# A decoder of four layers: softmax sums by part, gates in bfloat16 parts, and one named activation table set

## The reference, cut to what matters

```python
a_comp = _masked_softmax(q . compressed keys * SCALE, comp_mask)   # 32 blocks of 16 keys
a_sel  = _masked_softmax(q . keys of the top 2 blocks, causal_sel) # 16 keys
a_win  = _masked_softmax(q . keys, last 32 keys only)              # window
# _masked_softmax: e = exp(s - max), zeros where all is masked; e / sum(e)
g = softmax(x @ Wg + bg)
out = (g[0] * a_comp@cv + g[1] * a_sel@vs + g[2] * a_win@v) @ Wo + bo
```

```python
gates = zeros(T, 8); gates[rows, top2] = softmax(top2 logits)
h = relu(xf @ Wd[e] + bd[e]);  y = 0.5 * (h @ Wu[e] + bu[e])
out = einsum('te,ted->td', gates, y)
```

## Time and profile before

| | us |
|---|---|
| runs | 2310.97 to 2317.59, median of three 2312.99 |
| profiled execution | 2319.51 |
| its span | 2317.3 |
| PE / DVE / ACT / POOL busy | 1874.7 (81%) / 1637.3 (71%) / 1048.1 (45%) / 620.0 (27%) |
| DVE's scans of l3_attn, L2505, 128 of them | 193.7 busy, 1.1 idle before |
| granted PE clock over the span | 0.855 of full |

### The profile page before, as it was taken

How to read it: one execution, slowest core, us unless ns; L and a number is a source line. 1 busy time by engine, 2 the same in 40 slices (tenths; PEclk the granted TensorE clock), 3 DMA queues, 4 the chain that set the end, 5 groups by cost and what they waited for, 6 DMA issues and landing times. The chain is left out here.

```text
span 2317.3 us, 31149 instructions
## 1 busy us (share of the span) xinstructions
PE 1874.7 (81%) x11250; PEld 1074.1 (46%) x11250; DVE 1637.3 (71%) x3694; ACT 1048.1 (45%) x1706; POOL 620.0 (27%) x532
## 2 busy tenths in 40 slices
PE   4788888879888989999997668678976676689974
PEld 2444554536363333577776646555532232243432
DVE  6666847666678878744537896984379979994656
ACT  1226656474743553743434434442264355426552
POOL 0002424242332010100003544620136635731000
PEclk8888998989897786999998888776687797889975
DMA  4001213040302000000000000000000000000000
GB/s 171 1 0 41 65 29 77 9 97 2 89 17 95 1 1 1 1 23 1 1 1 10 1 1 1 1 1 1 1 0 1 1 0 0 1 1 1 1 1 19
DMA packets 19223, 44.31 MB, mean 19 GB/s; under 512 B 5323, under 2 KB 7935, under 8 KB 18047
## 3 DMA queue, kind: packets, MB, share of 16 engines
q1 hardware_dynamic: 19071, 42.33, 6.5%
HBM read 17.15 MB, written 1.05 MB: 8 GB/s over the span
## 5 line engine op out<-in xcount | busy, mean ns | idle before, releaser
L2374 PE MATMUL lane_banks<-l_attn_lane_hc,base 128*128 128x512 f32 x256 | 161.2, 743 | 91.6 <-DVE l_attn_lane_hc L2514 91.2
L2456 POOL TENSOR_TENSOR l_attn_lane_u<-l_attn_lane_xp,l_attn_lane_bn 128x512 f32<-128x512 f32 x128 | 189.6, 1510 | 123.9 <-ACT l_attn_lane_bn L2427 107.2
L604 POOL TENSOR_SCALAR lane_next_rstd<-lane_next_mv 128x4 f32<-128x4 f32 x48 | 11.9, 248 | 699.7 <-DVE lane_next_mv L581 699.7
L2505 DVE TENSOR_TENSOR_SCAN l_attn_lane_h<-l_attn_lane_da,l_attn_lane_u 128x512 f32<-128x512 f32 x128 | 193.7, 1558 | 1.1 <-ACT l_attn_lane_da L2435 0.8
L1728 ACT ACTIVATE l_ffn_lane_hT<-lane_banks,weights 128x512 f32<-128x512 f32 x128 | 87.9, 687 | 145.1 <-PE lane_banks L1682 144.5
L1774 DVE SCALAR_TENSOR_TENSOR l_ffn_lane_eo<-lane_banks,l_ffn_lane_sel,l_ffn_lane_eo 128x128 f32<-128x128 f32 x224 | 63.0, 343 | 101.4 <-PE lane_banks L1704 100.9
L2374 PEld LDWEIGHTS lane_banks<-l_attn_lane_hc,base 128*128 128x128 f32 x256 | 56.8, 238 | 162.5 <-DVE l_attn_lane_hc L2514 127.5
L1526 ACT ACTIVATE l_attn_lane_ex<-lane_banks 128x512 f32<-128x512 f32 x160 | 84.1, 668 | 97.2 <-PE lane_banks L1440 96.5
L1704 PEld LDWEIGHTS lane_banks<-weights,l_ffn_lane_hT 128*128 128x128 f32 x1024 | 119.8, 192 | 15.9 <-issue 12.2
L1704 PE MATMUL lane_banks<-weights,l_ffn_lane_hT 128*128 128x128 f32 x1024 | 122.8, 276 | 0.9 <-DVE l_ffn_lane_eo L1774 0.9
L591 DVE TENSOR_SCALAR lane_rows<-x,lane_next_mv,lane_next_rstd 128x128 f32<-128x128 f32 x192 | 76.0, 465 | 38.8 <-POOL lane_next_rstd L605 38.6
(11 more groups left out here) (528 smaller groups left out, 4719.6 us busy)
## 6 DMA issues: line engine op xcount, KB each, us to landing
f_attn_lane_vb<-f_attn_lane_work SPq DMA_DIRECT2D x192, 64.0 KB, 2.0
weights<-packed SPq DMA_DIRECT2D x1, 4564.5 KB, 13.5
f_attn_lane_work<-f_attn_lane_work SPq DMA_DIRECT2D x64, 64.0 KB, 2.0
f_attn_lane_vb<-f_attn_lane_va SPq DMA_DIRECT2D x8, 512.0 KB, 4.6
f_attn_lane_vb<-f_attn_lane_va SPq DMA_DIRECT2D x8, 384.0 KB, 5.9
weights<-packed SPq DMA_DIRECT2D x1, 2320.0 KB, 9.7
weights<-packed SPq DMA_DIRECT2D x1, 2091.0 KB, 14.1
weights<-packed SPq DMA_DIRECT2D x1, 1263.0 KB, 5.4
```

Of the source, the lines that this page charges most:

```text
L2374: pe.matmul(ps(2 + c), w("ident"), hc[:, c, :], start=(n == 1), stop=(n == NS)).then_inc(*s.up("state_added"))
L2456: g.tensor_tensor(u[:, i % 3, :], dtx[:, c, :], bn[:, n % 2, :], ALU.mult).then_inc(*s.up("u_ready"))
L2505: v.tensor_tensor_scan(h[:, c, :], da[:, i % 3, :], u[:, i % 3, :], 0.0, ALU.mult, ALU.add).then_inc(*s.up("scanned"))
```

## The change

In `l2_attn`, maxima, sums, subtraction and POOL's multiplication each go straight over the three parts of `sc` (64, 32 and 16 keys) in three instructions; the intermediate tiles of seven places are gone. The guard against an empty part is one `max` with 0.5 in place of an `is_equal` and an addition. The gate multiplication writes the weights in one instruction. `shift` waits for the subtraction of the group before, `weigh` for its weights.

In `l2_ffn`, the gates are split into three bfloat16 parts whose sum is the float32 value, transposed and copied out as 24 rows, and spread by a bfloat16 matmul over these. `gateT` stays for L2252.

In `f0_attn` and `l3_attn`, a named table set, which holds Ln and Exp, is loaded once in each unit. The costs in `Meter` have no price for it.

```diff
-A2_PARTS = ((0, 4), (4, 6), (6, 7))
+A2_PARTS = ((0, 64, 2), (64, 96, 0), (96, 112, 1))
 # l2_attn
+    def part(g, i):
+        lo, hi, k = A2_PARTS[i]
+        return sc[:, g % 2, :, :, lo:hi].rearrange("p j g n -> p (j g) n"), hi - lo, k
 # POOL, weights(g)
-            g_.tensor_tensor(sevenths(g), sevenths(g), bci(wt7[...], 16), ALU.mult)
+            for i in range(3):
+                to, n, k = part(g, i)
+                last = g_.tensor_tensor(to, to, bci(wt[:, g % 2, :, k], n), ALU.mult)
 # DVE, shift(g)
-            st.link(v.tensor_reduce(mx7[...], sevenths(g), AX.X, ALU.max))
-            for i, (lo, hi) in enumerate(A2_PARTS):
-                st.step(v.tensor_reduce(mx[:, :, i], mx7[:, :, lo:hi], AX.X, ALU.max))
+            if g >= 1:
+                v.wait_ge(*s.at("shifted", g))
+            for i in range(3):
+                of, _, k = part(g, i)
+                st.step(v.tensor_reduce(mx[:, :, k], of, AX.X, ALU.max))
             st.wait()
-            for i, (lo, hi) in enumerate(A2_PARTS):
-                st.step(v.tensor_scalar(mx7[:, :, lo:hi], bci(mx[:, :, i], hi - lo), -1.0e20, None, ALU.max))
-            st.wait()
-            v.tensor_tensor(sevenths(g), sevenths(g), bci(mx7[...], 16), ALU.subtract)
+            st.link(v.tensor_scalar(mx[:, :, :], mx[:, :, :], -1.0e20, None, ALU.max))
+            for i in range(3):
+                to, n, k = part(g, i)
+                last = v.tensor_tensor(to, to, bci(mx[:, :, k], n), ALU.subtract)
 # DVE, weigh(g)
-            (reduce of sevenths, three reduces, is_equal, add, reciprocal, three gate products, three copies)
+            if g >= 1:
+                v.wait_ge(*s.at("weights_ready", g))
+            for i in range(3):
+                of, _, k = part(g, i)
+                st.step(v.tensor_reduce(sm[:, :, k], of, AX.X, ALU.add))
+            st.wait()
+            st.link(v.tensor_scalar(zero[:, :, :], sm[:, :, :], 0.5, None, ALU.max))
+            st.link(v.reciprocal(sm[:, :, :], zero[:, :, :]))
+            yield
+            if g >= 2:
+                v.wait_ge(*s.at("probs_ready", g - 1))
+            v.tensor_tensor(wt[...], sm[...], gl[...], ALU.mult)
 # l2_ffn, PE
+        pe.wait_ge(*s.at("parts_ready", 1))
+        for t in range(NT):
+            last = pe.transpose(ps(1).bitcast(BF16)[0:3 * E, tile(t)], gate16[:, t, :, :], net.w16("ident16"))
+        last.then_inc(*s.up("partsT_in_psum"))
+        yield
+        pe.wait_ge(*s.at("partsT_ready", 1))
-            pe.matmul(ps(spread_bank[c]), w("pairpick", c * P, (c + 1) * P), gateT[:, :], start=True, stop=True)
+            pe.matmul(ps(spread_bank[c]), net.w16("pairpick16")[:, c * P:(c + 1) * P], gate16T[:, :], start=True, stop=True)
 # l2_ffn, ACT
+        act.wait_ge(*s.at("partsT_in_psum", 1))
+        act.activation(gate16T[:, :], ps(1).bitcast(BF16)[0:3 * E, 0:T], ACT.Copy).then_inc(*s.up("partsT_ready"))
 # l2_ffn, DVE
+        v.wait_ge(*s.at("gate_ready", 1))
+        st.link(v.tensor_copy(gate16[:, :, 0, :], gate[:, :, :]))
+        st.link(v.tensor_tensor(rest[:, :, :], gate[:, :, :], gate16[:, :, 0, :], ALU.subtract))
+        st.link(v.tensor_copy(gate16[:, :, 1, :], rest[:, :, :]))
+        v.tensor_tensor(gate16[:, :, 2, :], rest[:, :, :], gate16[:, :, 1, :], ALU.subtract).then_inc(*s.up("parts_ready"))
 # f0_attn, ACT, after the first Square; l3_attn, ACT, ahead of the first Exp
+                act.preload_act_table_set("natural_log_exp_and_others")
```

More of the change, by code:

```diff
@@ L127, in constants @@
     c["ident16"] = halfwords(np.eye(P))
+    c["pairpick16"] = halfwords(np.tile(np.kron(np.eye(8), np.ones((1, 64))), (3, 1)))
     c["later16"] = halfwords(np.where(p[None, :] <= p[:, None], 0.0, FAR))
@@ L1825, in l2_attn @@
     scale = A2_HD ** -0.5
-    seg7 = C // 16
     kp = sb("kp", [D, 32 + T])
@@ L2133, in shift @@
             v.wait_ge(*s.at("masked", GR * (g + 1)))
[L2134 to L2142 removed]
+            if g >= 1:
[3 more added lines that the diff above has]
+                st.step(v.tensor_reduce(mx[:, :, k], of, AX.X, ALU.max))
+            st.wait()
+            st.link(v.tensor_scalar(mx[:, :, :], mx[:, :, :], -1.0e20, None, ALU.max))
+            for i in range(3):
+                to, n, k = part(g, i)
+                last = v.tensor_tensor(to, to, bci(mx[:, :, k], n), ALU.subtract)
+            last.then_inc(*s.up("shifted"))
         def weigh(g):
@@ L2160, in weigh @@
                 v.wait_ge(*s.at("probs_ready", g - 1))
-            for i, (lo, hi) in enumerate(A2_PARTS):
-                last = v.tensor_copy(wt7[:, g % 2, :, lo:hi], bci(sm[:, :, i], hi - lo))
-            last.then_inc(*s.up("weights_ready"))
+            v.tensor_tensor(wt[:, g % 2, :, :].rearrange("p (j g) k -> p j g k", g=4), sm[:, :, :].rearrange("p (j g) k -> p j g k", g=4),
+                            gl[:, GR * g:GR * g + GR, :].unsqueeze(2).to_broadcast([P, GR, 4, 3]), ALU.mult).then_inc(*s.up("weights_ready"))
         def pick(g):
@@ L2213, in l2_ffn @@
     gateT = sb("gateT", [E, T])
+    rest = sb("rest", [P, NT, E])
+    gate16 = sb("gate16", [P, NT, 3, E], BF16)
+    gate16T = sb("gate16T", [3 * E, T], BF16)
     h = sb("h", [P, C, T])
@@ L2241, in tensor @@
         yield
+        pe.wait_ge(*s.at("parts_ready", 1))
+        for t in range(NT):
+            last = pe.transpose(ps(1).bitcast(BF16)[0:3 * E, tile(t)], gate16[:, t, :, :].rearrange("p i e -> p (i e)"), net.w16("ident16"))
+        last.then_inc(*s.up("partsT_in_psum"))
+        yield
+        pe.wait_ge(*s.at("partsT_ready", 1))
         pe.wait_ge(*s.at("gateT_ready", 1))
@@ L2244, in tensor @@
         for c in range(C):
-            pe.matmul(ps(spread_bank[c]), w("pairpick", c * P, (c + 1) * P), gateT[:, :], start=True, stop=True)\
+            pe.matmul(ps(spread_bank[c]), net.w16("pairpick16")[:, c * P:(c + 1) * P], gate16T[:, :], start=True, stop=True)\
               .then_inc(*s.up("spread_in_psum"))
@@ L3049, in transpose, with preload_act_table_set @@
         return self.work(0.06 + 0.0009 * width(out))
+    def preload_act_table_set(self, name):
+        self.log.append(("work", 0.0))
     def activation(self, out, in_, func, bias=0.0, scale=1.0, accum_out=None):
```

23 lines of the change are left out of this document (5 added, 18 removed).

## The result

| | before | changed |
|---|---|---|
| median, us | 2315.29 (2310.97 to 2323.7, 4 runs) | 2284.06 (2279.38 to 2285.97, 4 runs) |
| ratio of the runs | | 0.9842, 95% interval 0.9819 to 0.9866 |
| span of the profiled execution | 2317.3 | 2284.2 |

The kernel is 1.6% faster: 37 us by the ratio, 31 between these two medians, 33 between the two profiled executions. In the later runs of the experiments the median of the kernel before is 2318.9 to 2322.1, which fits the ratio better than the four runs of the table do. The forecast was -41 and 2272, its range 2248 to 2303.

What follows compares the result with a forecast made beforehand. DVE was taken to bound l2_attn's full stretches, PE l2_ffn, SP's DMA queue f0_attn, DVE's scans l3_attn. Savings 19 + 12 + 9 + 2.5 = 42.5, less 1.5 for replanning, gave -41: 2272 us from median 2312.99, range 2248 to 2303.

Steps and rivals of the forecast that it cites:

- l2_attn, forecast -19: l2_attn: DVE work 16.2 + 2.7 and stalls 7 saved, POOL costing 2, a fifth given back to waits: -19 us.
- The working of DVE's instructions: l2_attn: a shift falls from 4.92 to 4.58 us, a weigh from 4.12 to 3.1; 1.35 saved per group.
- I take a third of the 20.7 back: 7: l2_attn: of 20.7 us of DVE waiting in the two full stretches, 7 would be saved.
- the bound: l2_attn stalls, worst case: no waiting comes back and the added subtracts wait too, -12 us in place of 7 saved.
- Rival B: l2_attn: DVE's saved time turns into waits, so -19 becomes 0 and the kernel takes 2291 us; chance 0.17.
- E's mechanism: l2_attn: POOL's multiplies and DVE's subtracts wait for each other at the shared port; slower, 2331 us; chance 0.06.
- l2_ffn, forecast -12: l2_ffn: cheaper spread matmuls save 16 us, the added chain leaves 4 in the open: -12 us.
- not 16: l2_ffn: bf16 spread matmuls save 4.9 us on each of three rows and 1.3 on the fourth: -16.
- where 4 was put: l2_ffn: of 2.1 us added per row before the spread, half stays in the open, 1 per row: +4.
- Rival D: l2_ffn: less fp32 work lets PE's clock stand at full, 14 us in all, kernel at 2257 us; chance 0.10.
- Tables, forecast -9 and -2.5: Fewer ACT table loads: f0_attn's phases gain 9 us, mostly hidden behind SP's queue; l3_attn's two rows before the scans 2.5.

Runs made afterwards that it cites:

- e1: The l2_attn edit alone on the kernel before: 2288.18 us, ratio 0.986.
- e3: The named table sets of f0_attn and l3_attn alone on the kernel before: 2336.62 us, ratio 1.0079.
- e10: The changed kernel with POOL's spreads of the queries left out but for the first two of each row, order kept: 2258.42 us, ratio 0.9735 to the kernel before.
- e8: The changed kernel with one of four rotation DMAs per chunk of f0_attn issued from ACT's queue: 2269.07 us, ratio 0.9782 to the kernel before.
- e11: The changed kernel with two of four rotation DMAs per chunk of f0_attn issued from ACT's queue: 2275.43 us, ratio 0.9808 to the kernel before.
- e2: The l2_ffn edit alone on the kernel before: 2306.86 us, ratio 0.9958.
- e9: The kernel before with the added chain of l2_ffn, but the spread still a float32 matmul of gateT: 2325.81 us, ratio 1.0017.
- e6: The kernel before with both named table sets and six unneeded DVE reductions ahead of the last addition of row 3's l3_attn: 2317.44 us, ratio 0.9984.
- e5: The named table set in f0_attn alone on the kernel before: 2304.1 us, ratio 0.9944.
- e4: The changed kernel with DVE's subtraction and POOL's multiplication in l2_attn one instruction each again: 2280.42 us, ratio 0.9843 to the kernel before.

## Why the prediction was right, step by step

**Right sum, terms off both ways.** 2284 is 12 us over the forecast of 2272. l2_attn gave 9 us less than its term and l2_ffn 6 more, so that the sum came out this near is in part luck. So is the clock: had l3_xattn lost the 24 us that it lost in e1 and e3, the kernel would stand at about 2308, outside the range.

**l2_attn, forecast -19, measured -10** (-7 in e1). The working of DVE's instructions held to 0.05 us. The step that failed is "I take a third of the 20.7 back: 7": over all 16 groups the waits went from 21.5 to 27.5 instead of falling. I priced the added subtracts only in the bound. e10 shows what they wait for: the spreads. Of the 15.5 us that DVE's shifts and weighs gave up, 10 came out as time; the rest is in DVE's longer waits for ACT and PE (25.9 to 30.7, 10.6 to 15.7). Rival B, that it turns into waits, is in part true; E's mechanism is there, at 0.4 us more per group where 2.9 would have been needed. The size carries a scatter: with l2_attn untouched the stage had 310.8 to 311.4 in four traces and 305.9 in two, with the edit 299.0 to 304.2 in four (changed, e1, e8, e11). By the means of these, 309.3 and 301.9, the edit is worth 7.

**l2_ffn, forecast -12, measured -18** between the profiles, 14 in e2, 7.6 at full clock. The spread was worth 20.3, not 16, because it was priced at half clock and at 0.58 a matmul; three of its rows ran at or near full clock, and at half clock four matmuls take 1.86, not 2.3. The chain cost 2.5 (e9) where 4 was put. These two make up the 18, but part of them is the clock of the stage, which went from 0.68 to 0.72: hence the 7.6 at full clock. Rival D named that cause and its effect was thought to be all or nothing; the expert matmuls stayed at half in three rows, while the rest of the stage was granted more.

**Tables, forecast -9 and -2.5, measured -7 to -9 and at most -2.** The changed kernel is 8 us ahead at l1_attn and 7 at l2_attn; by the means of the traces without the set (777.0) and with it (767.7) it is 9. Most of ACT's 33 us were hidden, as forecast, since no more than this came out; that SP's queue was in the way is shown for the changed kernel by e8, where with these loads gone moving DMAs gave 11.5 to 16.5 more, and for the kernel before it is argued from that. In l3_attn the changed kernel gains 2 up to the last scan, but e6 against e5 gives 0.2 and e3 against the kernel before nothing: the scans set the pace, and the term of 2.5 was too large. I had not seen that the other lane's Sigmoid undoes the preload (ten loads, not eight). The Trainium skill ("ScalarE: Activation LUTs", What ACT_TABLE_LOAD costs) puts a drain of about 1.38 us beside each load, by its figure an estimated 36 us more of ACT for 26 loads. The trace shows no such drain (0.3 us of idle ahead of 17 loads); the gain of the phases, 6.4, cannot tell, as ACT's time is hidden there.

**What the prediction lacked.** It took the clock outside l2_ffn as given. Each of these kernels has stretches of about 50 us at half clock, and whether such a stretch falls on l3_xattn (24 us lost) or on the boundary behind it is worth more than most edits. e3's +18 is the example: a change that is still 6 us ahead behind the last stage that it touches, measured slower with an interval that excludes no change. The three edits measured alone give -32, -10 and +18, a sum of -24; measured in one kernel they give -37. What makes the clock fall at one place and not the other is not settled here; no run varied it alone.

## What to carry to other kernels

Where PE sets the pace, compare stages as length times granted clock before crediting an edit, and do it even when the interval of the times excludes no change; and look how far the same code moves between traces. When an engine's time is saved behind a queue of DMA issues, the queue is the next thing to move: one of four DMAs handed to an engine whose queue issues beside its work was worth 11.5 to 16.5 us here, 33 us of vanished table loads about 9. A long DVE operation cut in three can wait three times for a neighbour that is never idle: the longest group of three subtracts took 5.31 us for 2.16 of work, the longest single one 3.04 for 2.03. But making it one again moved the waits to the short operations (e4). Take away what is waited for, or count the waits and not only the elements.

## What the runs showed of the hardware

The granted clock can take two courses through the same matmuls: 0.79 and 1.12 us in the kernel before, 1.33 and 2.08 in e3, behind the same wait. Within one kernel the times spread by 20 us (before: 2305.22 to 2326.36 in 23 runs). Of DVE and POOL, the Trainium skill ("SBUF — State Buffer", Who interferes with whom) says that they exclude each other on a shared port pair. This case agrees: in e10 the subtracts' waits fell from 20.5 to 39.2 - 34.6 = 4.6 us when the spreads went, and no reduce of 1792 elements in the kernel before took more than 2.02. ACT's queue issued a DMA in 0.51 us while ACT computed (e8).
